# Attention stage: the gate's sum and the choice of experts at another key tile of a chunk, and the steps behind them moved along

## The reference

```python
src = x + _gqa(x, qw, qb, kw, kb, vw, vb, ow, ob)      # softmax(q k / sqrt(32)) v, 2048 keys
src = _rmsnorm(src, norm1_w)
logits = x_flat @ gate_w                               # 4096 x 8
probs = jax.nn.sigmoid(logits)
_, sel = jax.lax.top_k(probs, TOP_K)                   # 2 of 8
w_topk = w_topk / (jnp.sum(w_topk, axis=-1, keepdims=True) + 1e-06)
ranks = jnp.take_along_axis(jnp.cumsum(em, axis=0), flat_sel[:, None], axis=1)[:, 0] - 1
valid = ranks < capacity                               # 1280 rows for each expert
scatter_idx = jnp.where(valid, slot, N_EXPERTS * capacity)
```

## Time and profile before

| what | us |
|---|---|
| time before, median of 3 runs | 3303.2 (3293.76 to 3303.94) |
| the profiled execution, its own time | 3303.64 |
| its span (first to last instruction) | 3301.9 |
| attention's 31 units between first score products, about | 351 to 2167 |
| PE busy in the span | 3118.0 (94%) |
| POOL busy in the span | 2029.8 (61%) |

### The profile page before, as it was taken

How to read it: one execution, slowest core, us unless ns; L and a number is a source line. 1 busy time by engine, 2 the same in 40 slices (tenths; PEclk the granted TensorE clock), 3 DMA queues, 4 the chain that set the end, 5 groups by cost and what they waited for, 6 DMA issues and landing times. The chain is left out here.

```text
span 3301.9 us, 45552 instructions
## 1 busy us (share of the span) xinstructions
PE 3118.0 (94%) x16824; PEld 2013.7 (61%) x16824; DVE 2109.9 (64%) x3805; ACT 1608.9 (49%) x3249; POOL 2029.8 (61%) x880
## 2 busy tenths in 40 slices
PE   6998999999999999999999999984999999999992
PEld 4775444544544544545545545433999899889991
DVE  6887888788788778787787787813233333333334
ACT  3441466566656556565565665652333334334332
POOL 3443699899999989989899899992111111111114
PEclk8997799999999999999999999996999999999996
DMA  3665432001011022101101001012333333433237
GB/s 115 213 199 168 121 144 99 11 23 50 20 33 43 17 59 59 47 16 46 33 17 51 23 20 48 14 67 84 71 95 71 81 91 65 99 74 92 50 78 266
DMA packets 135521, 245.50 MB, mean 74 GB/s; under 512 B 30264, under 2 KB 35384, under 8 KB 132774
## 3 DMA queue, kind: packets, MB, share of 16 engines
q1 hardware_dynamic: 117232, 206.56, 19.5%
q0 software_dynamic: 16640, 35.42, 6.1%
q10 hardware_dynamic: 1461, 1.11, 0.1%
HBM read 127.82 MB, written 117.57 MB: 74 GB/s over the span
## 5 line engine op out<-in xcount | busy, mean ns | idle before, releaser
L1253 DVE TENSOR_REDUCE home_mxp<-p_ps_a 128x1 f32<-128x512 f32 x2021 | 1260.4, 680 | 281.8 <-PE p_ps_a L1452 272.7
L1172 ACT ACTIVATE p_PR<-p_ps_b 128x512 f32<-128x512 f32 x2048 | 1063.9, 604 | 704.8 <-PE p_ps_b L1466 692.8
L1033 POOL TENSOR_TENSOR p_PP<-p_PP,p_PR 128x2048 f32<-128x2048 f32 x223 | 1022.6, 4585 | 43.0 <-ACT p_PR L1172 20.0
L1452 PE MATMUL p_ps_a<-home_K,home_Q 96*128 96x512 f32 x2021 | 826.0, 436 | 19.6 <-DVE p_oh L1337 8.2
L1466 PE MATMUL p_ps_b<-home_Q,home_K 98*128 98x512 f32 x2048 | 784.9, 416 | 3.9 <-ACT p_PR L1172 3.7
L1029 POOL TENSOR_TENSOR p_PP<-p_PR 128x2048 f32<-128x2048 f32 x127 | 582.7, 4588 | 113.5 <-ACT p_PR L1172 102.6
L1731 POOL DMA_INDIRECT src_d<-p_YE,p_token x80 | 124.7, 1559 | 832.3 <-DVE p_YE L1857 622.6
L1452 PEld LDWEIGHTS p_ps_a<-home_K,home_Q 96*128 96x128 f32 x2021 | 383.8, 192 | 413.4 <-DVE home_mxp L1253 259.8
L1466 PEld LDWEIGHTS p_ps_b<-home_Q,home_K 98*128 98x128 f32 x2048 | 388.2, 190 | 234.9 <-ACT p_PR L1172 177.9
L1476 PE MATMUL p_ps_pv<-p_PR,p_VS 128*32 128x512 f32 x4096 | 522.4, 611 | 0.0
L1776 ACT ACTIVATE p_hf<-p_ps_h 128x384 f32<-128x384 f32 (+1 forms) x256 | 112.3, 439 | 576.3 <-PE p_ps_h L85 570.3
(11 more groups left out here) (194 smaller groups left out, 3261.7 us busy)
## 6 DMA issues: line engine op xcount, KB each, us to landing
weights_w_raw<-in_L_ffn_w SPq DMA_DIRECT2D x16, 2048.0 KB, 8.5
xe_d<-p_SR SPq DMA_DIRECT2D x20, 1056.0 KB, 10.1
home_Q<-qh_d SPq DMA_DIRECT2D x64, 256.0 KB, 3.8
p_XE<-xe_d SPq DMA_DIRECT2D x16, 792.0 KB, 4.6
src_d<-p_SR SPq DMA_DIRECT2D x9, 1024.0 KB, 6.3
p_XE<-xe_d SPq DMA_DIRECT2D x16, 528.0 KB, 3.7
p_X<-in_x SPq DMA_DIRECT2D x8, 1024.0 KB, 7.8
x_d<-p_x SPq DMA_DIRECT2D x8, 1024.0 KB, 5.3
```

What stands on the lines that cost most here:

```text
L1033: nc.gpsimd.tensor_tensor(PP[:, buf, :, :], PP[:, buf, :, :], PR[:, tile_at(u, tile), :, :], ALU.add).then_inc(add_made, 1)
L1172: nc.scalar.activation(PR[:, tile_at(u, kt), j, :], ps_b[:, n % BK, :], ACT.Exp, scale=SCALE).then_inc(ex_made, 1)
L1253: nc.vector.reduce_max(mxp[:, a // (S // CH), a % (S // CH):a % (S // CH) + 1], ps_a[:, bank, :], AXX).then_inc(a_read, 1)
L1452: nc.tensor.matmul(ps_a[:, bank, :], QS[u % QK][0:96, j, t * P:(t + 1) * P], KS[u % KV][0:96, kb * CH:(kb + 1) * CH], start=True, stop=Tru ...
```

## The change

Nothing is added or removed; every step of the routing of the chunk before runs at another place in each engine's order. The letter `N` goes from the end of key tile 1 of unit 2 to the end of key tile 11 of unit 2 (beginning in the second chunk), and `K` from key tile 8 of unit 2 to key tile 0 of unit 3. On ACT and DVE the four small steps go along; they are now given as (unit, key tile), since two of them fall into unit 3. On POOL `weigh` goes from behind addition 2 to behind addition 10 of unit 2, `rank` from behind addition 5 of unit 2 to behind addition 0 of unit 3, `finish` from behind addition 8 of unit 2 to behind addition 2 of unit 3, and the four sends of unit 3 from behind additions 1, 3, 5, 7 to behind 3, 5, 7, 8. The late sends stay. The tail after the last chunk is not touched.

```diff
-    EXTRA = {0: {11: "O", 13: "O", 15: "O"}, 1: {1: "O", 10: "R", 11: "R", 12: "R", 13: "R"}, 2: {0: "L", 1: "N", 8: "K"}, 3: {}}
+    EXTRA = {0: {11: "O", 13: "O", 15: "O"}, 1: {1: "O", 10: "R", 11: "R", 12: "R", 13: "R"}, 2: {0: "L", 11: "N"}, 3: {0: "K"}}
...
-    WEIGH_AT, RANK_AT, FINISH_AT = (2, 2), (2, 5), (2, 8)
-    EXP_AT, INVERT_1_AT, INVERT_2_AT, SUM_AT = 1, 3, 7, 12
-    SENDS = {(3, 1): 0, (3, 3): 1, (3, 5): 2, (3, 7): 3}
+    WEIGH_AT, RANK_AT, FINISH_AT = (2, 10), (3, 0), (3, 2)
+    EXP_AT, INVERT_1_AT, INVERT_2_AT, SUM_AT = (2, 12), (2, 13), (3, 1), (3, 4)
+    SENDS = {(3, 3): 0, (3, 5): 1, (3, 7): 2, (3, 8): 3}
...
-                        if g == 2 and not first and kt == EXP_AT:
+                        if (g, kt) == EXP_AT and not first:
                             sigmoid_exp(c - 1)
...
-                        if g == 2 and not first:
-                            if kt == INVERT_1_AT:
-                                invert_sigmoids(c - 1)
-                            if kt == INVERT_2_AT:
-                                invert_sums(c - 1)
-                            if kt == SUM_AT:
-                                sum_chosen(c - 1)
+                        if (g, kt) == INVERT_1_AT and not first:
+                            invert_sigmoids(c - 1)
+                        if (g, kt) == INVERT_2_AT and not first:
+                            invert_sums(c - 1)
+                        if (g, kt) == SUM_AT and not first:
+                            sum_chosen(c - 1)
```

## The result

The changed kernel takes 3305.19 us (median of 20 runs, 3299.08 to 3309.74) against 3299.51 for the kernel before (median of 20, 3292.12 to 3304.68). The ratio is 1.0017, 95% interval 1.001 to 1.0023: 5.7 us slower by the medians, clear of noise and about half of what I forecast. The profiled execution took 3307.33 us, with a span of 3305.6.

The account below looks back on a forecast made before the run. PE was taken to set the pace, with POOL right beside it in unit 3. The terms -18.8 + 1.2 + 1.2 + 16.8 + 11.6 - 1.5 gave +10.5 us, so 3313.7 us, range 3298 to 3323.

Parts of the forecast that it names:

- N leaves key tile 2 without a stall: Unit 2, key tile 2, chunks 1 to 6: the stall and the clock falls behind it go, -18.8 us.
- POOL is not late at the start of unit 3: Unit 3: without rank and finish in unit 2, addition 0 starts 0.14 us behind key tile 1's last exponential, -0.75 us.
- stall moved: Rival: key tile 12 stalls for N, or a DVE step of unit 3 waits for POOL; 3320 to 3333 us, chance 0.10.
- no wait: Rival: PE reaches the D of key tile 15 in unit 3 after addition 8 ends; 3281 to 3295 us, chance 0.12.
- the clock stays: Rival: PE's wait at the D in unit 3 comes but the clock holds; 3298 to 3307 us, chance 0.16.
- The sign: Whole kernel: slower 0.45, same 0.42, faster 0.13.
- N at key tile 11: Unit 2, key tile 11: no stall, 0.2 us more than in key tile 1 for a wait on a read, +1.2 us.
- POOL in unit 3: Unit 3, D of key tile 15: PE waits 3.1 us for addition 8 in place of 0.29, chunks 1 to 6, +16.8 us.
- "K" and DVE's steps: K goes from unit 2 to unit 3 at the same price; DVE's moved small steps cost 0.2 us a chunk, +1.2 us.
- The last chunk: Last chunk: unit 3's addition 0 starts 5.0 us earlier, POOL's chain grows 3.6 us; -1.4, taken as -1.5 us.
- The clock: Behind the D's wait in unit 3: the clock falls in five or six of six chunks, 5.5 x 2.1 = +11.6 us.

Follow-up runs that it names:

- pool_alone: Changed kernel with N, K, sigmoid_exp and invert_sigmoids put back as before, so only POOL's part and DVE's two dependent steps move; ratio 1.0076 to the kernel before.
- sends_later: Changed kernel with no sends left in unit 3, all eight moved into units 0, 1 and 2 of the next chunk; ratio 0.9925 to the kernel before.
- filled kernels: Changed kernel and kernel before, each with an A product repeated (13 and 6 times) to fill PE's wait; ratios 0.9979 and 0.9958 to the kernel before.
- before_sends_later: Kernel before with only its sends moved out of unit 3 into the next chunk's units 0, 1 and 2; ratio 0.9986 to the kernel before.
- filled kernel before: Kernel before with the second A of key tile 2 in unit 2 made 6 times, filling PE's 1.17 us wait; ratio 0.9958, 3286.23 us.
- before_again: Kernel before run once more with no edit; ratio 0.9999 to the kernel before, median 3299.98 us.
- send_two: Changed kernel with two sends ahead of addition 8 in place of three, the other six in the next chunk; ratio 0.9985 to the kernel before.

## Why the prediction was half right

**Right, by its own steps.** N leaves key tile 2 without a stall (-18.8 us, 31.69 against 31.68), and does not stall PE in key tile 12. ACT's wait at line 1200 in the loop is gone. POOL is not late at the start of unit 3, `rank` (3.11 us from 1227.69 to 1230.80) and `finish` (1.56) cost what the earlier trace rows gave, the D of key tile 15 waits in each of chunks 1 to 6, and the clock falls behind it in most of them. pool_alone and sends_later show the two halves with opposite signs, the rival "stall moved" and the rival "no wait" are out, and "the clock stays" is out as well, since it fell in four to six chunks. The sign was right. The measured medians lie in the stated range.

**Wrong: the size, +10.5 us against 5.7.** With the filled kernels the sum can be split into a part with the clock held and a part of the clock. My sum has +9.3 for the first (10.8 in chunks 1 to 6, -1.5 in the last) and +1.2 for the second. Measured are 6.0 to 6.3, and -1 to -3.

- *The term "N at key tile 11".* I took +0.2 us for each chunk over the old place, for a wait on a read. It was -0.3: 0.61 us there against 0.90 in key tile 1. Six times 0.5 is 3.1 us of the miss, and this is the step that failed most. The wait on a read did not come: PE is busy for all of both key tiles. And 0.90 is what N costs in key tile 1, not what it costs anywhere; its eight products take 1.06 us there and 0.95 in key tile 11. Why the place makes the rest of the difference is not shown.
- *The term "POOL in unit 3".* The wait is 2.73 us on average and not 3.1. Before, PE waited 0.2 to 0.4 in five chunks and not in the sixth, so the growth is 2.5 and not 2.8: 1.9 us of the miss. In chunk 3 both ends of it were off a little. POOL takes 3.4 us more from addition 0 to the end of addition 8 and not 3.6, and PE reaches the D 47.4 us behind the exponentials of key tile 1 and not 47.2.
- *The term "K" and DVE's steps.* I took +1.2. Where no D waits (sends_later against before_sends_later) units 3 and 0 grow by 3.4 us in six chunks, and 2.9 of that is K's own price, which unit 2 saves: +0.5.
- *The last chunk*: from the start of unit 2 to the last D it was 113.13 us before (2108.90 to 2222.03) and 111.27 after (2114.45 to 2225.72), -1.9 against -1.5. Part of this is a fall at key tile 2 before; in the filled pair it is -0.4, 1.1 us less gain than I had.
- *The clock.* My +11.6 was to stand against the 10.4 within the -18.8. Filling measures 11 to 13 after and 14 before by the ratios. So the term was of the right size, and the net effect of the clock on the change is -1 to -3 us, not +1.

Chunk by chunk with the clock held, unit 2 fell by 2.2 us (58.46 in the filled kernel before, 56.25) where I had 1.4 - 0.2 + 0.5 for K = 1.7, and units 3 and 0 rose by 3.3 (117.4 to 120.7, means of the six in the filled pair) where I had 3.5. Six times the difference is +6.7, where mine was 6 x 1.8 = 10.8. The terms above would make it still smaller: some 0.3 us for each chunk in units 3 and 0 is not assigned, and part of that is the fill itself (0.4 us in chunk 2).

**What cannot be settled.** I set my sum on one execution of 3303.64 us, which lies 4.1 us over the median of the 20. The patterns of the falls differ between any two profiles, also outside the change: the first B of chunk 0's attention came 3 us earlier in the changed kernel's profile, and unit 0 of chunk 1 5 us earlier, so the two spans differ by less than the changed stretch does (1418.70 to 1429.33 us, +10.6). In the second pair of profiles that stretch grows by 8.1. By the first pair alone the forecast would look nearly right (10.6 - 1.9 = 8.7 us against 10.5), where the medians and the filled pair say 6. Why the clock falls behind 1.17 us in one chunk and holds behind 2.27 in another is open. My row with a wait of 2.20 and the clock at 1.00 was one draw: in before_again the clock fell for 3.4 us at that same place.

## What to carry to other kernels

A step taken out of PE's way has to be paid in the queue that it moves into. Look for the one instruction ahead of which that queue has no room left (here a D that already waited 0.29 us for POOL), and move work to behind it, not to ahead of it. Here the place of the sends, three indirect DMAs of one microsecond ahead of that D, decided between a loss of 0.15% and a gain of 0.8% (of which the sends alone are 0.14%). Where a wait of PE can't be removed, repeating the last product through it held the clock in both kernels. It costs nothing as long as the repeats are no longer than the wait. And an effect of 0.2% wants the part with the clock held separated from the part of the clock, by such a fill, before its terms are believed.

## What the runs showed of the hardware that I had not expected

- Short waits are enough for a fall, but not always. Behind PE's wait of 1.17 us in key tile 2 the clock fell to 0.50 in 5, 4, 4 and 1 of six chunks (the kernel before twice, before_sends_later, pool_alone); at the D, with 1.2 to 1.9 us, in 3 of six (send_two), and with 2.2 to 3.2 us in 5, 4 and 6 of six. With no wait over 0.4 us it fell in none of the 24 chunks of sends_later, its repeat and the two filled kernels. A fall in chunks 1 to 6 lasts 3.4, 6.8 or 10.2 us and costs 1.3 to 1.7, 2.8 to 3.1 or 3.9 to 4.3 us. The Trainium skill (TensorE: Matmul & The Clock Gate, "A second HAM failure mode: psum-queue depth-cycling") has micro-idles between matmul groups that cost re-throttling; the trace agrees for the wait on a bank in key tile 2, the wait at the D is one for POOL and does the same, and the fill of the idle time took all of it away in chunks 1 to 6.
- The pattern of falls can repeat from chunk to chunk within one execution, or not. In pool_alone the six at the D began at 795.7, 1034.6, 1273.5, 1512.5, 1751.4 and 1990.3 us, each time 238.9 apart and each 3.4 us long. In the changed kernel's first profile their lengths were 10.2, none, 10.2, 3.4, 10.2 and 3.4 us. What sets the pattern is not shown.
